# The gated unit of layer 0 in three passes of rounded and rest parts, its context loaded a batch ahead and split on GpSimd

## The chip, the core and the metric

One core of a Trainium2 chip runs the whole program. The metric is the device time of one execution in microseconds. A barrier stands between the stages of the program. TensorE (PE), VectorE (DVE), ScalarE (ACT), GpSimd (POOL) and SyncE (SP, which issues DMAs) each work through their own instructions in order and wait for one another by semaphores.

## What is computed

Two decoder layers on x of 4 batches x 512 rows x 256 features. Each layer has self-attention, a second unit over a context and a mixture of experts, each after a layer norm and added to x. In layer 0 the second unit is no attention. It is a gated unit whose three weights are all the context of the batch:

```python
def _L0_xattn_ref(x, w1, v1, w2):
    x1 = jnp.einsum('eth,efh->etf', x, w1)
    x2 = jnp.einsum('eth,efh->etf', x, v1)
    h = jax.nn.gelu(x1, approximate=True) * x2
    return jnp.einsum('etf,efh->eth', h, w2)
...
x = x + _L0_xattn_ref(_layernorm(x, axis=-1), ctx_1024, ctx_1024, ctx_1024)
```

Since w1 and v1 are the same, x1 = x2 is computed once: g = norm(x) times context transposed (512 x 256 by 256 x 512), h = gelu(g) * g, and h times context (512 x 512 by 512 x 256), for each batch.

## The kernel before

`geglu` (L805) is this unit. P is 128; a batch has NT = 4 tiles of rows, CC = 2 chunks of features and FC = 4 chunks of context rows. Features lie on partitions for the first product, context rows for the second.

One batch goes through these kinds of step, which `run` hands to each engine in the same order:

- IN: SP loads `ctxT` (the context transposed, 512 KB) and `ctxN` (the context, 512 KB) from memory, each into its only buffer. `ctxT` waits until the batch before has read it (`g_ready`), `ctxN` likewise (`y_ready`).
- LN: VectorE takes statistics and mean and variance (L978, L985). GpSimd makes the inverse deviation with two 128x4 operations (`inverse_deviation`, L968 and L970). VectorE scales the four row tiles into `xn` (L991).
- T: TensorE transposes `xn` into PSUM `t_ps` (L935), and VectorE copies that to `xnT` (L907).
- G: TensorE makes the four chunks of `g_ps` in 32-bit products (L945), two per chunk. ScalarE takes the GELU of a chunk (L921), VectorE multiplies it with g into `h` (L895).
- Y: TensorE makes the output in two halves j of two row tiles, four 32-bit products each (L956). VectorE adds a half to x (L900).

The order is LN and T of batch 0, and then for each batch b: IN(b), G(b), LN(b+1), Y(b,0), T(b+1), Y(b,1). The first three batches are a hardware loop (`batch_body`, L69), whose waits compare with values held in registers; the last follows it as straight code. So the rows of the next batch are normalised and transposed beside the output products, and everything on an engine behind a waiting instruction waits too.

The mixture of experts (`experts`, L1344) already works in three passes: each 32-bit operand is held as a rounded part (hi, type fp32r) and a rest (lo = value - hi), and hi*hi + lo*hi + hi*lo is accumulated (L1686). ScalarE rounds there (L1560) and VectorE subtracts (L1607). The tile tag `l0g` marks this unit, `l0a` the attention before it, `l0ms` and `l0m` the experts after it, and `l1a`, `l1x`, `l1m` those of layer 1.

## Time and profile before

| | us |
|---|---|
| median of 3 runs | 2181.52 |
| lowest and highest run | 2175.15, 2187.56 |
| span of the profiled execution | 2182.9 |
| of it: first attention and load of constants | 0 to 380.9 |
| of it: the gated unit, barrier to last add | 380.9 to 463.4 |
| TensorE, VectorE, ScalarE, GpSimd busy over the span | 1766.8, 1336.3, 953.7, 360.1 |

The times list holds only the three runs; the profiled execution has its span, which lies 1.4 us above their median. A busy time of an engine is a sum over stages with different limits, so the share of 81% for TensorE says little about one stage. The windows of the stage and its timeline tell which wait ends last there. A matmul's record includes the time the result takes through the array, so the distance between two starts, not the duration, is what one costs in a row of them; a 32-bit product stands in the trace as two records.

### The profile page before, as it was taken

What the parts mean: (1) busy time and instruction counts of PE and PEld (TensorE: products, weight loads), DVE (VectorE), ACT (ScalarE), POOL (GpSimd) and SP (SyncE); (2) the same over time, 40 slices, a digit from 0 to 9 for tenths busy, and PEclk for the clock granted to TensorE, in tenths of its full rate; (3) what the DMA queues carried; (4) which work ended last, traced back from release to release, by engine and by line L of the source; (5) the groups of instructions that cost most, each with busy time, mean ns of one, the idle gap of its engine ahead of it and who ended that gap; (6) DMA issues with size and microseconds to landing.
All of it is one profiled execution on the core that took longest, in us unless ns stands there. A gap on an engine that the chain in (4) does not pass through costs nothing. (4 is left out here: it accounts for less than half of the span.)

```text
span 2182.9 us, 35377 instructions
## 1 busy us (share of the span) xinstructions
PE 1766.8 (81%) x11104; PEld 1317.3 (60%) x11104; DVE 1336.3 (61%) x2397; ACT 953.7 (44%) x1769; POOL 360.1 (16%) x560
## 2 busy tenths in 40 slices
PE   4999998773979993399999958788762599999990
PEld 2566665463969993145555523333332599999990
DVE  4565663443458883577677546756874377777762
ACT  1243343111346661035455515755851366666640
POOL 4122120015000004422112022111103200000005
PEclk9799998876989996679999968988985799999995
DMA  3121110243047773212112013111104466666634
GB/s 111 35 48 42 31 45 1 58 159 104 3 131 231 231 227 96 72 40 51 31 29 58 2 51 80 46 46 39 34 1 137 142 205 208 211 210 204 206 98 120
DMA packets 193808, 211.51 MB, mean 97 GB/s; under 512 B 28723, under 2 KB 172469, under 8 KB 193717
## 3 DMA queue, kind: packets, MB, share of 16 engines
q1 hardware_dynamic: 178356, 174.71, 26.7%
q0 software_dynamic: 15360, 35.68, 6.1%
q8 instruction: 46, 0.75, 0.1%
q14 instruction: 46, 0.37, 0.1%
HBM read 143.71 MB, written 28.57 MB: 79 GB/s over the span
## 5 line engine op out<-in xcount | busy, mean ns | idle before, releaser
L1686 PE MATMUL l1m_xg_ps<-l1m_sb_xrows_hi,l1m_sb_hi 128*128 128x256 f32 x736 | 209.5, 285 | 1.4 <-DVE l1m_sb_xrows_lo L1601 1.4
L1686 PE MATMUL l1m_xg_ps<-l1m_sb_xrows_hi,l1m_sb_lo 128*128 128x256 f32 x736 | 209.2, 284 | 0.0
L1686 PE MATMUL l1m_xg_ps<-l1m_sb_xrows_lo,l1m_sb_hi 128*128 128x256 f32 x736 | 209.2, 284 | 0.0
L590 ACT ACTIVATE l1x_sb_probs<-l1x_s_ps,l1x_sb_kmax 128x512 f32<-128x512 f32 x256 | 173.6, 684 | 72.9 <-DVE l1x_sb_kmax L524 47.2
L493 DVE TENSOR_REDUCE l1a_sb_mx<-l1a_a_ps 128x1 f32<-128x512 f32 x256 | 169.2, 686 | 55.8 <-PE l1a_a_ps L666 55.1
L524 DVE TENSOR_REDUCE l1x_sb_kmax<-l1x_s_ps 128x2 f32<-128x1024 f32 x128 | 156.1, 1220 | 62.2 <-PE l1x_s_ps L693 61.8
L493 DVE TENSOR_REDUCE l0a_sb_mx<-l0a_a_ps 128x1 f32<-128x128 f32 (+3 forms) x256 | 116.4, 486 | 90.3 <-PE l0a_a_ps L669 88.3
L596 ACT ACTIVATE l1a_sb_probs<-l1a_s_ps 128x1024 f32<-128x1024 f32 x128 | 130.5, 1022 | 89.8 <-PE l1a_s_ps L693 89.3
L1686 PEld LDWEIGHTS l1m_xg_ps<-l1m_sb_xrows_hi,l1m_sb_hi 128*128 128x128 f32 x736 | 142.4, 193 | 1.8 <-DVE l1m_sb_xrows_lo L1601 1.8
L1686 PEld LDWEIGHTS l1m_xg_ps<-l1m_sb_xrows_hi,l1m_sb_lo 128*128 128x128 f32 x736 | 142.3, 193 | 0.0
L1686 PEld LDWEIGHTS l1m_xg_ps<-l1m_sb_xrows_lo,l1m_sb_hi 128*128 128x128 f32 x736 | 142.3, 193 | 0.0
L596 ACT ACTIVATE l0a_sb_probs<-l0a_s_ps 128x1024 f32<-128x1024 f32 (+3 forms) x128 | 89.6, 701 | 119.6 <-PE l0a_s_ps L696 118.9
L1607 DVE TENSOR_TENSOR l1m_sb_lo<-l1m_sb_raw,l1m_sb_hi 128x512 fp32r<-128x512 f32 x184 | 118.8, 687 | 32.5 <-ACT l1m_sb_hi L1560 30.6
L666 PE MATMUL l1a_a_ps<-l1a_sb_kst,l1a_sb_qst 96*128 96x512 f32 x256 | 130.2, 521 | 9.9 <-DVE l1a_sb_mx L493 7.3
L1560 ACT ACTIVATE l1m_sb_hi<-l1m_sb_raw 128x512 fp32r<-128x512 f32 x184 | 104.9, 620 | 16.4 <-DMA l1m_sb_raw<-in_l1m_w 15.3
L712 PE MATMUL l1x_o_ps<-l1x_sb_probs,l1x_sb_vaug 128*32 128x512 f32 x512 | 76.3, 670 | 42.8 <-DVE l1x_sb_vaug L540 42.6
L1686 PE MATMUL l1m_xy_ps<-l1m_sb_hi,l1m_sb_xh_hi 128*128 128x256 f32 x368 | 106.8, 290 | 2.8 <-issue 2.8
L1686 PE MATMUL l0m_xg_ps<-l0m_sb_xrows_hi,l0m_sb_hi 128*128 128x256 f32 x368 | 105.4, 286 | 3.1 <-DVE l0m_sb_xrows_lo L1601 3.1
L1686 PE MATMUL l0m_xg_ps<-l0m_sb_xrows_hi,l0m_sb_lo 128*128 128x256 f32 x368 | 105.1, 285 | 0.0
L1686 PE MATMUL l0m_xg_ps<-l0m_sb_xrows_lo,l0m_sb_hi 128*128 128x256 f32 x368 | 105.0, 285 | 0.0
L1686 PE MATMUL l1m_xy_ps<-l1m_sb_hi,l1m_sb_xh_lo 128*128 128x256 f32 x368 | 104.7, 285 | 0.0
L1686 PE MATMUL l1m_xy_ps<-l1m_sb_lo,l1m_sb_xh_hi 128*128 128x256 f32 x368 | 104.7, 285 | 0.0
(341 smaller groups left out, 4577.4 us busy)
## 6 DMA issues: line engine op xcount, KB each, us to landing
l1m_sb_raw<-in_l1m_w SPq DMA_DIRECT2D x184, 256.0 KB
l0m_sb_raw<-in_l0m_w SPq DMA_DIRECT2D x96, 256.0 KB
l1m_sb_raw<-in_l1m_w SPq DMA_DIRECT2D x23, 1024.0 KB
l0m_sb_raw<-in_l0m_w SPq DMA_DIRECT2D x24, 512.0 KB, 4.0
rows_dram<-const_zeros SPq DMA_DIRECT2D x1, 5888.0 KB, 22.9
l0m_sb_xrows<-rows_dram SPq DMA_DIRECT2D x23, 256.0 KB, 4.3
outs_dram<-l0m_sb_xy SPq DMA_DIRECT2D x23, 256.0 KB, 2.7
l1m_sb_xrows<-rows_dram SPq DMA_DIRECT2D x23, 256.0 KB, 3.9
```

What stands on the lines that cost most here:

```text
L493: dve.tensor_reduce(mx[:, g, qt, h:h + 1], a_ps[:, u % 2, 0:last], AX.X, ALU.max).then_inc(a_max.sem, 1)
L524: dve.tensor_reduce(kmax[:, n % 4, :], scores[buffer_of(n)][:, :, :], AX.X, ALU.max, negate=True).then_inc(kmax_done.sem, 1)
L590: ins = act.activation(probs[:, n % 8, e, :], scores[buffer_of(n)][:, e, :], ACT.Exp, bias=kmax[:, n % 4, e:e + 1], accum_out=zsum[:, n % ...
L596: act.activation(probs[:, n % 8, :, c0:T], scores[buffer_of(n)][:, :, c0:T], ACT.Exp, scale=SCALE).then_inc(exp_done.sem, 1)
L666: ins = pe.matmul(at, qst[h % 2][0:96, h // 2, qt * P:(qt + 1) * P], kst[0:96, h // 2, 0:last], start=True, stop=not causal)
L712: ins = pe.matmul(o_ps[32 * i:32 * i + 32, c0:T], vaug[:, kt, GH * g + i, :], probs[:, (8 * g + 2 * kt + i // 2) % 8, i % 2, c0:T], start= ...
L1560: ins = act.activation(two_chunks(hi, k % 2, f), two_chunks(raw13, n, f), ACT.Copy)
L1607: ins = dve.tensor_tensor(two_chunks(lo, k % 2, f), two_chunks(raw13, n, f), two_chunks(hi, k % 2, f).bitcast(F32), ALU.subtract)
L1686: ins = pe.matmul(at, s, m, start=n == 0, stop=n == len(passes) - 1)
```

## The change

In layer 0's gated unit every 32-bit product becomes three passes over fp32r parts.

- `xnT`, `h`, `ctxT` and `ctxN` each get a hi and a lo tile. ScalarE rounds (`xnT_hi` from PSUM, `h_hi` from `h`), VectorE subtracts (`xnT_lo` in place of the copy, `h_lo`).
- The context's tiles are double. Batch b + 2 is loaded after G(b) in the order, and as soon as the raw tile of batch b has been split. GpSimd splits both context tiles: cast, subtract, cast, subtract, of 128x1024 each.
- Batches 0 and 1 are split where IN stands, batch 0 ahead of LN(0) and batch 1 right behind it. Later ones are split behind the second output half, which on GpSimd is right behind the pair of LN(b+1).
- The loop over batches is gone; all four stand as straight code.
- ScalarE's table for GELU is loaded once instead of at each turn of the loop.

The diff, cut to its core:

```diff
@@ geglu: the order @@
+            step("IN", 0)
             step("LN", 0)
+            step("IN", 1)
             step("T", 0)
-            def body(b, nxt):
-                step("IN", b)
+            for b in range(B):
                 step("G", b)
-                if nxt is not None:
-                    step("LN", nxt)
+                if b + 2 < B:
+                    step("IN", b + 2)
+                if b + 1 < B:
+                    step("LN", b + 1)
                 step("Y", b, 0)
...
-            batch_body(eng, B, body)
@@ sync @@
-                wait_all(sp, (g_ready, b - 1, FC - 1))
...
+                if b >= 2:
+                    ctx_low.wait(sp, b - 2, 0)
+                sp.dma_start(ctxT[:, b % 2, :, :], w["ctxT"][b].rearrange("(c p) t -> p c t", p=P)
+                             ).then_inc(ctxT_in[b % 2], 16)
+                if b >= 2:
+                    ctx_low.wait(sp, b - 2, 1)
+                sp.dma_start(ctxN[:, b % 2, :, :], w["ctx"][b].rearrange("(c p) d -> p c d", p=P)
+                             ).then_inc(ctxN_in[b % 2], 16)
@@ gpsimd @@
+            def split(b):
+                k = b % 2
+                pool.wait_ge(ctxT_in[k], (b // 2 + 1) * 16)
+                if b >= 2:
+                    g_ready.wait(pool, b - 2, FC - 1)
+                pool.tensor_copy(ctxT_hi[:, k, :, :], ctxT[:, k, :, :]).then_inc(ctx_high.sem, 1)
+                ctx_high.wait(pool, b, 0)
+                pool.tensor_tensor(ctxT_lo[:, k, :, :], ctxT[:, k, :, :], ctxT_hi[:, k, :, :].bitcast(F32),
+                                   ALU.subtract).then_inc(ctx_low.sem, 1)
+                pool.wait_ge(ctxN_in[k], (b // 2 + 1) * 16)
+                if b >= 2:
+                    y_ready.wait(pool, b - 2, 1)
...
+            run(pool, {"LN": lambda b: inverse_deviation(pool, b, mv, rstd, const, ln_stats, ln_rstd, xn_done),
+                       "Y": lambda b, j: split(b + 2) if j == 1 and b + 2 < B else None,
+                       "IN": lambda b: split(b) if b < 2 else None})
@@ vector @@
+            def rest(b, f):
+                h_high.wait(dve, b, f)
+                dve.tensor_tensor(h_lo[:, f, :], h[:, f, :], h_hi[:, f, :].bitcast(F32), ALU.subtract
+                                  ).then_inc(h_low.sem, 1)
...
                     dve.tensor_tensor(h[:, f, :], g_ps[:, f, :], gelu[:, f, :], ALU.mult).then_inc(h_done.sem, 1)
+                    if f:
+                        rest(b, f - 1)
+                rest(b, FC - 1)
...
-                    dve.tensor_copy(xnT[:, c, :], t_ps[:, c, :]).then_inc(t_read.sem, 1)
+                    xnT_high.wait(dve, b, c)
+                    dve.tensor_tensor(xnT_lo[:, c, :], t_ps[:, c, :], xnT_hi[:, c, :].bitcast(F32), ALU.subtract
+                                      ).then_inc(t_read.sem, 1)
@@ scalar @@
+            def high(b, f):
+                h_done.wait(act, b, f)
+                y_ready.wait(act, b - 1, 1)
+                act.activation(h_hi[:, f, :], h[:, f, :], ACT.Copy).then_inc(h_high.sem, 1)
...
+                    act.activation(xnT_hi[:, c, :], t_ps[:, c, :], ACT.Copy).then_inc(xnT_high.sem, 1)
@@ tensor @@
+            def three_passes(at, chunks):
+                passes = [(s[a], m[b]) for s, m in chunks for a, b in ((0, 0), (1, 0), (0, 1))]
+                for n, (s, m) in enumerate(passes):
+                    ins = pe.matmul(at, s, m, start=n == 0, stop=n == len(passes) - 1)
+                return ins
...
-                pe.wait_ge(ctxT_in, (b + 1) * 16)
+                ctx_low.wait(pe, b, 0)
...
-                    pe.wait_ge(ctxN_in, (b + 1) * 16)
-                    h_done.wait(pe, b, FC - 1)
+                    ctx_low.wait(pe, b, 1)
+                    h_low.wait(pe, b, FC - 1)
```

GpSimd at the start of the unit, before: the pair of batch 0, then the loop (L72 and L57 are the loop's and the waits' own instructions) with the pair of the next batch.

```order
L880 UNCONDITIONAL_BRANCH
L968 TENSOR_TENSOR l0g_sb_rstd<-l0g_sb_mv,const_eps 128x4
L970 TENSOR_TENSOR l0g_sb_rstd<-l0g_sb_rstd,const_minus_half 128x4
L72 UNCONDITIONAL_BRANCH
L72 ISA
L57 ISA
L968 TENSOR_TENSOR l0g_sb_rstd<-l0g_sb_mv,const_eps 128x4
L57 ISA
L970 TENSOR_TENSOR l0g_sb_rstd<-l0g_sb_rstd,const_minus_half 128x4
```

The same place of the changed kernel: the splits of batches 0 and 1, and the pairs of batches 0 and 1.

```order
L903 CAST l0g_sb_ctxT_hi<-l0g_sb_ctxT 128x1024
L905 TENSOR_TENSOR l0g_sb_ctxT_lo<-l0g_sb_ctxT,l0g_sb_ctxT_hi 128x1024
L910 CAST l0g_sb_ctxN_hi<-l0g_sb_ctxN 128x1024
L912 TENSOR_TENSOR l0g_sb_ctxN_lo<-l0g_sb_ctxN,l0g_sb_ctxN_hi 128x1024
L1035 TENSOR_TENSOR l0g_sb_rstd<-l0g_sb_mv,const_eps 128x4
L1037 TENSOR_TENSOR l0g_sb_rstd<-l0g_sb_rstd,const_minus_half 128x4
L903 CAST l0g_sb_ctxT_hi<-l0g_sb_ctxT 128x1024
L905 TENSOR_TENSOR l0g_sb_ctxT_lo<-l0g_sb_ctxT,l0g_sb_ctxT_hi 128x1024
L910 CAST l0g_sb_ctxN_hi<-l0g_sb_ctxN 128x1024
L912 TENSOR_TENSOR l0g_sb_ctxN_lo<-l0g_sb_ctxN,l0g_sb_ctxN_hi 128x1024
L1035 TENSOR_TENSOR l0g_sb_rstd<-l0g_sb_mv,const_eps 128x4
L1037 TENSOR_TENSOR l0g_sb_rstd<-l0g_sb_rstd,const_minus_half 128x4
```

Four operations of 128x1024 have come ahead of the first pair, and four between it and the second.

VectorE through G and LN, before, in the last (straight) batch and the add behind it: four multiplies in a row, and nothing after them but the adds. In the loop the same four stand ahead of the statistics of the next batch.

```order
L72 REGISTER_ALU
L72 COMPARE_AND_BRANCH
L895 TENSOR_TENSOR l0g_sb_h<-l0g_g_ps,l0g_sb_gelu 128x512 x4
L900 TENSOR_TENSOR x_sb<-l0g_y_ps,x_sb 128x512 x2
L808 UNCONDITIONAL_BRANCH
```

Changed, G(0) and LN(1) on VectorE:

```order
L935 TENSOR_TENSOR l0g_sb_h<-l0g_g_ps,l0g_sb_gelu 128x512 x2
L926 TENSOR_TENSOR l0g_sb_h_lo<-l0g_sb_h,l0g_sb_h_hi 128x512
L935 TENSOR_TENSOR l0g_sb_h<-l0g_g_ps,l0g_sb_gelu 128x512
L926 TENSOR_TENSOR l0g_sb_h_lo<-l0g_sb_h,l0g_sb_h_hi 128x512
L935 TENSOR_TENSOR l0g_sb_h<-l0g_g_ps,l0g_sb_gelu 128x512
L926 TENSOR_TENSOR l0g_sb_h_lo<-l0g_sb_h,l0g_sb_h_hi 128x512 x2
L1045 BN_STATS l0g_sb_stats<-x_sb 128x6 x4
L1050 MEMSET l0g_sb_nothing 128x1
L1052 BN_AGGR l0g_sb_mv<-l0g_sb_stats 128x2 x4
L1058 TENSOR_SCALAR l0g_sb_xn<-x_sb,l0g_sb_mv,l0g_sb_rstd 128x256 x4
```

Each chunk's subtraction stands behind the next chunk's multiply, and the last two stand ahead of the statistics and scalings of the next batch. On TensorE the unit had 64 products and transposes as code (8 transposes, a loop body of 32, 24 after it) and has 320 now (4 times 8 + 24 + 48).

## Rows read from the trace of the kernel before

**Rows 1.** Windows of the unit: busy us (x instructions) by engine, PEclk, DMA share, GB/s

```profile
387.10:395.90 8.80, 7.91 (x15) 4.09 (x16) 1.43 (x3) 1.88 (x2) 0.00 (x0) 0.50 0.00 1
395.90:463.60 67.70, 56.69 (x210) 36.88 (x208) 29.34 (x69) 11.31 (x17) 3.62 (x6) 1.00 0.17 47
```

**Rows 2.** Chain that ended last, in order of time: start, us, what

```profile
1812.95 8.64 PE l1m_xg_ps L1686 x72
```

**Rows 3.** Timeline of turn 1: start, us, engine, line, operation, count, [idle before <-releaser]

```profile
411.19 7.03 PE L945 MATMUL l0g_g_ps<-l0g_sb_xnT,l0g_sb_ctxT 128*128 128x512 f32 x16
418.33 0.60 ACT L921 ACTIVATE l0g_sb_gelu<-l0g_g_ps 128x512 f32<-128x512 f32 x1 [1.12 <-PE l0g_g_ps L945]
419.57 1.39 DVE L978 BATCH_NORM_STATS2 l0g_sb_stats<-x_sb 128x6 f32 x4
419.79 3.72 PE L956 MATMUL l0g_y_ps<-l0g_sb_ctxN,l0g_sb_h 128*128 128x256 f32 x16 [1.57 <-DVE l0g_sb_h L895]
424.72 1.09 PE L935 MATMUL l0g_t_ps<-const_ident,l0g_sb_xn 128*128 128x128 f32 x8 [1.22 <-DVE l0g_sb_xn L991]
429.10 7.03 PE L945 MATMUL l0g_g_ps<-l0g_sb_xnT,l0g_sb_ctxT 128*128 128x512 f32 x16
```

**Rows 4.** Timeline, start and end of the unit

```profile
382.35 0.43 SPq L873 DMA_DIRECT2D l0g_sb_ctxT<-in_ctxT  x1
384.28 0.20 POOL L968 TENSOR_TENSOR l0g_sb_rstd<-l0g_sb_mv,const_eps 128x4 f32<-128x4 f32 x1 [70.68 <-DVE l0g_sb_mv L985]
384.56 1.03 POOL L970 TENSOR_TENSOR l0g_sb_rstd<-l0g_sb_rstd,const_minus_half 128x4 f32<-128x4 f32 x1
385.69 1.38 DVE L991 TENSOR_SCALAR l0g_sb_xn<-x_sb,l0g_sb_mv,l0g_sb_rstd 128x256 f32<-128x256 f32 x4 [1.49 <-issue]
389.96 10.10 PE L945 MATMUL l0g_g_ps<-l0g_sb_xnT,l0g_sb_ctxT 128*128 128x512 f32 x16 [0.86 <-DVE l0g_sb_xnT L907]
401.63 3.72 PE L956 MATMUL l0g_y_ps<-l0g_sb_ctxN,l0g_sb_h 128*128 128x256 f32 x16 [1.57 <-DVE l0g_sb_h L895]
455.50 7.14 PE L956 MATMUL l0g_y_ps<-l0g_sb_ctxN,l0g_sb_h 128*128 128x256 f32 x32 [1.46 <-issue]
462.69 0.69 DVE L900 TENSOR_TENSOR x_sb<-l0g_y_ps,x_sb 128x512 f32<-128x512 f32 x1 [2.76 <-PE l0g_y_ps L956]
```

**Rows 5.** Groups by line (count, busy, mean ns, idle), then one DMA issue group (us to landing)

```profile
L1560 ACT ACTIVATE l1m_sb_hi<-l1m_sb_raw 128x512 fp32r<-128x512 f32 x184 | 104.9, 620 | 16.4 <-DMA l1m_sb_raw<-in_l1m_w 15.3
L413 POOL TENSOR_TENSOR l1a_sb_vaug<-l1a_sb_v,l1a_sb_bv 128x256 f32<-128x256 f32 x16 | 11.8, 740 | 3.9 <-PE l1a_o_ps L712 2.7 <-issue 1.0
L387 POOL MEMSET l1a_sb_vaug<- 128x2048 f32 x1 | 1.8, 1837 | 0.1
...
l0g_sb_ctxT<-in_ctxT SPq DMA_DIRECT2D x4, 512.0 KB, 3.6
```

**Rows 6.** Timeline, GpSimd and VectorE, start of the first layer and at 1120 us

```profile
12.85 3.50 POOL L383 MEMSET l0a_sb_qst<- 128x4096 f32 x1
12.98 9.32 DVE L450 TENSOR_SCALAR l0a_sb_xn<-x_sb,l0a_sb_mv,l0a_sb_rstd 128x256 f32<-128x256 f32 x4 [1.51 <-issue]
...
1119.96 1.46 POOL L413 TENSOR_TENSOR l1a_sb_vaug<-l1a_sb_v,l1a_sb_bv 128x256 f32<-128x256 f32 x2
1119.74 1.84 DVE L450 TENSOR_SCALAR l1a_sb_xn<-x_sb,l1a_sb_mv,l1a_sb_rstd 128x256 f32 x2
```

**Rows 7.** Timeline of TensorE: longest and shortest of the five gaps

```profile
1395.31 1.23 PE L712 MATMUL l1x_o_ps<-l1x_sb_probs,l1x_sb_vaug 128*32 128x512 f32 x8 [3.22 <-DVE l1x_sb_vaug L540]
...
2122.99 0.44 PE L1686 MATMUL l1m_xy_ps<-l1m_sb_hi,l1m_sb_xh_hi 128*128 128x256 f32 x1 [2.85 <-issue]
```

**Rows 8.** Windows behind those two gaps

```profile
1395.80:1402.40 6.60, 6.50 (x29) 2.80 (x21) 4.69 (x9) 5.53 (x16) 2.53 (x5) 0.52 0.26 65
2123.20:2126.40 3.20, 3.20 (x16) 3.20 (x16) 0.00 (x0) 0.00 (x0) 0.00 (x0) 0.50 0.00 0
```

**Rows 9.** Waits of TensorE: line, cause, us in total, times, longest

```profile
PE l0ms_xg_ps L1686 <- issue: 19.7, 16, 2.4
```

More of the change, by code:

```diff
@@ L822, in geglu @@
         xn = sb("xn", [P, NT, D])
-        xnT = sb("xnT", [P, CC, T])
-        ctxT = sb("ctxT", [P, CC, T])
-        ctxN = sb("ctxN", [P, FC, D])
+        xnT_hi, xnT_lo = (sb(n, [P, CC, T], F32R) for n in ("xnT_hi", "xnT_lo"))
+        ctxT = sb("ctxT", [P, 2, CC, T])
+        ctxN = sb("ctxN", [P, 2, FC, D])
+        ctxT_hi, ctxT_lo = (sb(n, [P, 2, CC, T], F32R) for n in ("ctxT_hi", "ctxT_lo"))
+        ctxN_hi, ctxN_lo = (sb(n, [P, 2, FC, D], F32R) for n in ("ctxN_hi", "ctxN_lo"))
         gelu = sb("gelu", [P, FC, T])
         h = sb("h", [P, FC, T])
+        h_hi, h_lo = (sb(n, [P, FC, T], F32R) for n in ("h_hi", "h_lo"))
         nothing = sb("nothing", [P, 1])
@@ L832, in geglu @@
         y_ps = ps("y_ps", [P, 2, 2, D])
-        ctxT_in = ctx.enter_context(nc.semaphore(f"{tag}_ctxT_in"))
-        ctxN_in = ctx.enter_context(nc.semaphore(f"{tag}_ctxN_in"))
+        ctxT_in = [ctx.enter_context(nc.semaphore(f"{tag}_ctxT_in{k}")) for k in range(2)]
+        ctxN_in = [ctx.enter_context(nc.semaphore(f"{tag}_ctxN_in{k}")) for k in range(2)]
         ln_stats = steps("ln_stats", 2 * NT)
@@ L921, in gate, with transposed @@
                     act.activation(gelu[:, f, :], g_ps[:, f, :], ACT.Gelu_apprx_tanh).then_inc(g_gelu.sem, 1)
-            run(act, {"G": gate})
+                    if f:
+                        high(b, f - 1)
+                high(b, FC - 1)
+            def transposed(b):
+                for c in range(CC):
+                    t_ready.wait(act, b, c)
+                    g_ready.wait(act, b - 1, FC - 1)
+                    t_read.wait(act, b - 1, c)
+                    act.activation(xnT_hi[:, c, :], t_ps[:, c, :], ACT.Copy).then_inc(xnT_high.sem, 1)
+            run(act, {"G": gate, "T": transposed})
         @block.tensor
@@ L943, in hidden @@
                     h_done.wait(pe, b - 1, f)
[L944 to L947 removed]
+                    cols = slice(f * P, (f + 1) * P)
+                    three_passes(g_ps[:, f, :], [((ctxT_hi[:, b % 2, c, cols], ctxT_lo[:, b % 2, c, cols]),
+                                                  (xnT_hi[:, c, :], xnT_lo[:, c, :])) for c in range(CC)]
+                                 ).then_inc(g_ready.sem, 1)
             def output(b, j):
                 if j == 0:
[L951 to L952 removed]
+                    ctx_low.wait(pe, b, 1)
+                    h_low.wait(pe, b, FC - 1)
                 x_added.wait(pe, b - 1, j)
                 for t in range(2):
[L955 to L957 removed]
+                    rows = slice((2 * j + t) * P, (2 * j + t + 1) * P)
+                    ins = three_passes(y_ps[:, j, t, :], [((h_hi[:, f, rows], h_lo[:, f, rows]),
+                                                           (ctxN_hi[:, b % 2, f, :], ctxN_lo[:, b % 2, f, :]))
+                                                          for f in range(FC)])
                 ins.then_inc(y_ready.sem, 1)
```

37 lines of the change are left out of this document (17 added, 20 removed).

## The prediction

> **What bounds the kernel now.** The kernel is a chain of stages with a barrier between them, so a microsecond won or lost inside one stage shows in full at the end unless a later wait takes it up. I first read the windows of the gated unit [rows 1], then a whole turn of its loop in the timeline [rows 3], then its start and end [rows 4]. The unit fills 380.9 to 463.4 us, 82.5 of 2182.9 us. From 395.9 us on TensorE's clock is 1.00, the 2.4 GHz level; before that it is 0.50. One turn runs from 411.19 to 429.10 us, 17.91 us, and TensorE sets most of it. The hidden products take 7.03 us. Then it waits 1.57 us for the last GELU and product, and starts the first half of the output products at 419.79. It next waits 1.22 us for the normalised rows of the next batch (transposes at 424.72), and does the second output half [rows 3]. GpSimd has little to do here: two tiny operations per batch, the second 1.03 us long, yet every batch's transposes wait behind them [rows 4].
>
> **The products.** A 32-bit hidden product appears as two records, 16 for a batch in 7.03 us. In three passes it is 24 of 512 columns. In the experts, which already work in three passes, a 256-column pass costs 8.64/72 = 0.120 us [rows 2]. One of 512 columns costs twice that at most, 0.24, and half a 32-bit record of the same width, 7.03/16/2 = 0.22, is the nearest row below [rows 3]. I take 0.22: 24 x 0.22 = 5.3 us; with 0.24 it would be 5.8, and the gate chain below ends no later than 0.2 us after. The output is 48 passes of 256 columns, 5.76 us, where 32 records took 7.14 [rows 4]. Alone that would save 1.7 + 1.4 us a batch, 12 us in all. What follows takes it back.
>
> **Gate chain.** Before, the last product of a group is followed by one GELU (0.60) and one multiply (0.69). Now a rounding copy on ScalarE (0.62) and a subtraction on VectorE (0.69) follow [rows 3, 5], and each engine does two operations per chunk. VectorE's pace is then 2 x 0.69 = 1.38 us plus hops, about 1.42, against TensorE's 1.32. Stepping through the four chunks from the start of G, with the result read 0.28 us after the last pass: results at 1.6, 2.9, 4.3, 5.6; last multiply ends 7.2, last rounding 7.8, last rest 8.6. Output begins at 8.7 us. Before it was 419.79 - 411.19 = 8.60 [rows 3]. So the quicker hidden products buy nothing (+0.1), and TensorE now stands idle about 3.2 us there instead of 1.57. The saved output half before the transposes buys nothing either: they wait for normalised rows, which follow the gate chain. Only the half after them shortens: 429.10 - 424.72 = 4.39 becomes 0.93 + 2.88 = 3.81, a gain of 0.6 a turn.
>
> **The split stands ahead of the first normalisation.** In GpSimd's order four 128x1024 operations now precede the 1/deviation of batch 0. The nearest rows are its 128x256 add, 740 ns, and its 128x2048 memset, 1837 ns [rows 5]. The 128x4 add takes 0.20 us (0.28 from 384.28 to 384.56), so the add grows by (0.74 - 0.20)/252 = 2.15 ns per element and a subtraction of 1024 is 2.45 us. A cast has one input: at the memset's 0.9 ns it is 0.95 us, at the adding rate 2.45. I take 1.3, nearer the memset. The context is issued at 382.35 and lands 3.6 to 3.9 us later, 386.2 [rows 4, 5]. Then 2 x (1.3 + 2.45) + gaps 0.3 + the pair 1.3 ends at 395.3, against 385.59 before: **+9.7 us**. Bounds: 0.95 and 2.2 give +8.5; all four at 3.0 give +14.2.
>
> By the Trainium skill (GPSIMD Engine Reference, section Elementwise — side-by-side cycle accounting) a two-input operation on 2048 elements takes 4497 ns there, which as an estimate is 2.25 us for 1024. With it the sum below would be 1.2 us lower. No run so far shows a 1024-element operation.
>
> **GpSimd holds VectorE.** At the first layer's start, four VectorE scalings of 128x256 take 9.32 us, though one takes 0.35 to 0.41 alone. Beside them GpSimd runs memsets one after another, the first of 3.50 us and a later one of 1.84 [rows 4 to 6]. At 1119.74 two scalings take 1.84 us beside two GpSimd adds [rows 6]. This is the same operation as `xn`, from the same kind of operands. In the new order a split stands right behind the pair of batch 0, 1 and 2, and its inputs are there by then, so it starts with the scalings. Batch 0 meets all four operations (7.5 us + 0.4 instead of 1.38): **+6.5**. Batches 1 and 2 meet cast and subtraction of ctxT; the ctxN half waits for output that itself waits for these rows: 3.75 + 0.1 + two free scalings 0.7 + the tail 0.35 = 4.9 instead of 1.38, **+3.5** each. Batch 3 meets none. The bound below is 0 if VectorE always gets in first; above, with 3.0 us operations, +11 and +5.9.
>
> **Clock.** In stretches at 1.00, idle gaps of TensorE of 1.6 us did not lower it. The five gaps from 2.85 to 3.22 us all did: two of them with the clock behind are shown [rows 7, 8]. It stays at 0.50, the 1.2 GHz level, for over 3 us after work resumes at 2122.99 and for some 7 at 1395.31 [rows 7, 8]. The new 3.2 us gap and, in turns 0 and 1, some 4 us before the transposes are such gaps. A fall in the first output half is covered by the wait for the rows. A fall at the transposes or in the last output is not: 4 us at half speed do 2 us of work, **+2.0**, three times.
>
> **Sum, against the profile's own time.** To the first output: +9.7 + 6.5, one more hop through ScalarE between transposes and products +0.6, and the first hidden products, partly at the low clock both times, with their chain 10.95 instead of 401.63 - 389.96 = 11.67 [rows 4], -0.7: **+16.1**. Turns 0 and 1: 3.5 + 2.0 - 0.6 + 0.1 = 5.0 each, **+10.0**. Turn 2: -0.6 + 0.1 = **-0.5**. End: 463.38 - 455.50 = 7.88 becomes 5.76 + 0.36 + 0.69 + 2.0 = 8.8, **+0.9**. Total +26.5 us. The three dropped table loads (1.28 us) lay behind running products in the loop and cost or give nothing; the first one stays. The earlier context loads are hidden both times after batch 0. The span of 2182.9 stands 1.4 above the median of the runs, so the sum gives 2181.5 + 26.5 = **2208 us**.
>
> **Rivals.**
> *A dear cast* (0.13). If casts and subtractions take 3.0 us each, the bounds above add 4.5 + 4.5 + 2 x 2.4 = 14: 2222 us. For it: a rounding copy may be software work per element; against it: the memset's rate.
> *No holding* (0.10). If only memsets and adds into that buffer hold VectorE, or it always gets in first, 6.5 + 7.0 and the two clock falls at the transposes go, 17.5 less: 2190.5 us. Against it stands the 1.84 us beside adds [rows 6].
> *Not slower, by a stall that moves* (0.10). In the next stage TensorE waits 19.7 us in 16 gaps for nothing the profile shows, between 525 and 550 us, while GpSimd scatters rows [rows 9]. The unit's straight code grows from 64 to 320 TensorE products and transposes, which shifts all code behind it. If the stall depends on where the code lies, it can go: with the clock's part of it 22 us, 2208 - 22 = 2186. It decides from the point where less than 12 us of the terms above remain or more than 15 of the stall goes. Against it: it begins and ends with the scatter, which moves along unchanged. It could also grow, by up to the scatter's remaining 20 us.
> The Trainium skill (Runtime: NRT & Kernel Launch, section Instruction fetch mechanics) says that instructions are refilled in blocks of 256, so a shift of the code moves the block ends; it also advises unrolling over loops. No row shows a wait at the end of the present loop, so by the trace the unrolling gives nothing here.
>
> **Numbers.** The forecast has 0.60 with 2200 to 2216 as its own range, the rivals 0.13, 0.10 and 0.10; 0.07 is left for gains I can't name, such as a gate chain that hides better. Leaving out what lies beyond them on both sides, the range is 2190 to 2222. A measurement of this kernel can tell some 0.5% (11 us) from no change: slower needs over 2192.4. Slower by more: 0.60 + 0.13 and 0.02 of the others, 0.75. Within: *no holding* and most of the moved stall, 0.20. Faster by more: 0.05, if the stall goes and nothing holds VectorE.
>
> **What would show it.** The first pair of 128x4 operations of the unit should end near 395 us after the four splits; `l0g_sb_xn` should have a median near 0.4 us but a maximum of several us, for batches 0 to 2 alone; TensorE's gap before the first output product should be 3.0 to 3.3 us, with the clock at 0.50 behind it; the unit should last about 109 us. The forecast falls if the cast takes under 1 us and the scalings keep 0.41 us, or if the waits between 525 and 550 us change.

## The result and the profile after

| | before | after |
|---|---|---|
| median, us (10 runs each, timed in turn) | 2186.69 | 2200.04 |
| lowest and highest, us | 2175.15, 2192.97 | 2196.68, 2206.14 |
| span of the profiled execution, us | 2182.9 | 2197.8 |
| the unit, us | 83.2 | 102.4 |

The changed kernel is slower: ratio 1.0076, 95% interval 1.0056 to 1.0095, which is 12 to 21 us. Over ten runs the kernel before has a median 5.2 us above that of the three runs that the forecast started from, so the medians differ by 13.4 us. "The unit" is measured here and below from the start of the last addition of the attention before it (L516 on VectorE) to the end of the unit's own last addition. It grew by 19.2 us where the forecast had 26.5. All splits, holds and clock falls that the prediction named are there, most of them smaller.

The start, from the timeline of the changed kernel (start, us, engine, line, operation, count, idle before and its releaser). It answers [rows 4]:

```profile
387.19 1.04 POOL L903 CAST l0g_sb_ctxT_hi<-l0g_sb_ctxT 128x1024 fp32r<-128x1024 f32 x1 [69.35 <-DMA l0g_sb_ctxT<-in_ctxT]
388.30 2.34 POOL L905 TENSOR_TENSOR l0g_sb_ctxT_lo<-l0g_sb_ctxT,l0g_sb_ctxT_hi 128x1024 fp32r<-128x1024 f32 x1
...
394.28 1.03 POOL L1037 TENSOR_TENSOR l0g_sb_rstd<-l0g_sb_rstd,const_minus_half 128x4 f32<-128x4 f32 x1
395.28 1.03 POOL L903 CAST l0g_sb_ctxT_hi<-l0g_sb_ctxT 128x1024 fp32r<-128x1024 f32 x1
395.40 6.94 DVE L1058 TENSOR_SCALAR l0g_sb_xn<-x_sb,l0g_sb_mv,l0g_sb_rstd 128x256 f32<-128x256 f32 x4 [9.74 <-issue]
...
402.39 1.97 PE L994 MATMUL l0g_t_ps<-const_ident,l0g_sb_xn 128*128 128x128 f32 x8 [20.87 <-DVE l0g_sb_xn L1058]
```

The split starts when the context lands, four operations pass, and the pair of 128x4 operations ends at 395.31. The next split starts at once, beside the four scalings, which take 6.94 us instead of 1.38. TensorE sits idle for 20.87 us.

A turn is the time from one batch's first output product to the next's. The first line below is of the kernel before, where the scalings of the next batch take 1.38 us and start 3.64 us behind their statistics (419.57 in [rows 3]); the others are the same part of turn 0 in the changed kernel:

```profile
423.21 1.38 DVE L991 TENSOR_SCALAR l0g_sb_xn<-x_sb,l0g_sb_mv,l0g_sb_rstd 128x256 f32 x4 [1.51 <-POOL l0g_sb_rstd L970]
...
416.75 0.36 PE L1002 MATMUL l0g_y_ps<-l0g_sb_ctxN_hi,l0g_sb_h_hi 128*128 128x256 f32 x1 [2.85 <-issue]
419.71 1.03 POOL L903 CAST l0g_sb_ctxT_hi<-l0g_sb_ctxT 128x1024 fp32r<-128x1024 f32 x1
419.85 4.12 DVE L1058 TENSOR_SCALAR l0g_sb_xn<-x_sb,l0g_sb_mv,l0g_sb_rstd 128x256 f32<-128x256 f32 x4 [1.47 <-issue]
420.82 2.34 POOL L905 TENSOR_TENSOR l0g_sb_ctxT_lo<-l0g_sb_ctxT,l0g_sb_ctxT_hi 128x1024 fp32r<-128x1024 f32 x1
424.02 1.55 PE L994 MATMUL l0g_t_ps<-const_ident,l0g_sb_xn 128*128 128x128 f32 x8 [2.67 <-DVE l0g_sb_xn L1058]
```

Two gaps stand here, 2.85 us ahead of the output and 2.67 ahead of the transposes; batch 1 has the same again (2.85, 2.66 and scalings of 4.12 us), batches 2 and 3 only the gap ahead of the output. Windows behind them (columns as in [rows 1]) show the clock; those of before are 1.00 in the same two places:

```profile
417.80:421.30 3.50, 3.50 (x18) 3.35 (x16) 1.99 (x8) 0.00 (x0) 2.68 (x4) 0.53 0.01 2
424.50:427.70 3.20, 3.20 (x17) 3.20 (x16) 1.45 (x3) 1.19 (x2) 0.00 (x0) 0.50 0.00 0
```

TensorE's issue waits in the experts stage, which answer [rows 9], hardly changed:

```profile
PE l0ms_xg_ps L1753 <- issue: 18.5, 14, 3.2
```

### The profile page after: what moved, and what is told of

It is laid out like the page before. It is cut to its first block and busy times, and to the rows that moved or that the text cites. A ratio compares the mean times of both kernels' runs of the same rounds, so it can differ in the third digit from the quotient of the medians.

```text
span 2197.8 us, 35505 instructions
## 1 busy us (share of the span) xinstructions
PE 1759.5 (80%) x11200; PEld 1327.4 (60%) x11200; DVE 1356.9 (62%) x2413; ACT 964.0 (44%) x1791; POOL 387.9 (18%) x576
## 5 line engine op out<-in xcount | busy, mean ns | idle before, releaser
L712 PE MATMUL l1x_o_ps<-l1x_sb_probs,l1x_sb_vaug 128*32 128x512 f32 x512 | 75.3, 662 | 42.1 <-DVE l1x_sb_vaug L540 41.8
```

Of the source, the lines that this page charges most:

```text
L712: ins = pe.matmul(o_ps[32 * i:32 * i + 32, c0:T], vaug[:, kt, GH * g + i, :], probs[:, (8 * g + 2 * kt + i // 2) % 8, i % 2, c0:T], start= ...
```

## Experiments

Theory: the loss is (a) the split ahead of the first pair, (b) GpSimd's large operations holding VectorE's scalings, (c) the clock behind the gaps; the saved products buy little because the gate chain sets the output's start. The rivals: no holding, a gap that has nothing to do with the split, a stall elsewhere that moves. Each experiment starts from the changed kernel unless it says otherwise. e1 to e4 ran on one chip (before 2184.67 us), e5 to e7 on a second (2152.75), e8, e6 again, e9 and e10 on a third (2178.65), e11 on a fourth (2183.47).

### e1: the first pair ahead of the split

```diff
-            step("IN", 0)
             step("LN", 0)
+            step("IN", 0)
             step("IN", 1)
```

> The changed kernel with one swap in the common order: LN(0) stands ahead of IN(0), so GpSimd makes the 1/deviation of batch 0 before it splits any context. Theory 1 (the split ahead of the pair and its holding of VectorE cost the start 13.8 us): the pair no longer waits for the context, which lands about 4.3 us after the last add of the attention plus 1.3; the first cast starts with the second scaling, so the four scalings still take about 5 us (one of them free), and the products of batch 0 start some 10 us earlier than in the changed kernel: the unit takes 91 to 92 us instead of 101.7, the turns stay at 21.1, 21.0 and 16.8 us. Rival (the start is late because the products must wait for the split context in any order): the products of batch 0 start no more than 2 us earlier and the unit keeps over 99 us.

Unit 92.4 us, 10.0 less. The first hidden product came 10.3 us earlier.

```profile
383.52 1.03 POOL L1037 TENSOR_TENSOR l0g_sb_rstd<-l0g_sb_rstd,const_minus_half 128x4 f32<-128x4 f32 x1
384.65 4.92 DVE L1058 TENSOR_SCALAR l0g_sb_xn<-x_sb,l0g_sb_mv,l0g_sb_rstd 128x256 f32<-128x256 f32 x4 [1.48 <-issue]
384.79 1.16 POOL L903 CAST l0g_sb_ctxT_hi<-l0g_sb_ctxT 128x1024 fp32r<-128x1024 f32 x1 [0.24 <-DMA l0g_sb_ctxT<-in_ctxT]
```

The pair ends 8.3 us earlier, measured from the start of the unit. The other 2.0 us come from a shorter hold (4.92 us for 6.94), because the first scaling starts ahead of the first cast and is free. So the place of the split costs 8.3 us, and the scalings are held as soon as a split stands beside them. The whole time was 2201.15 in one run, no lower than that of the changed kernel: layer 1's two attention stages took 733.9 us in that execution and 720.3 in the changed kernel's. The experiments are therefore read from the unit first; e9 and e10 are about this.

### e2: a split waits for the scalings

```diff
                 k = b % 2
+                if b:
+                    xn_done.wait(pool, b - 1, NT - 1)
                 pool.wait_ge(ctxT_in[k], (b // 2 + 1) * 16)
```

> The changed kernel, but GpSimd starts the split of batch 1, 2 and 3 only when VectorE has finished scaling the rows of the batch before (a wait on xn_done added, the order kept). Theory 1 (GpSimd's operations hold VectorE's scalings, and the late rows then let the clock fall): the four scalings take 1.4 us for every batch, 5.6 us less at the start and 2.7 less in turns 0 and 1; the gap before the transposes goes below 2 us, the clock stays up there, and turns 0 and 1 come down from 21.1 to about 16.8 us. The unit takes 87 to 88 us instead of 101.7. Rival (the scalings are slow for another reason, such as the context's DMAs writing into SBUF beside them): they keep 6.9 and 4.1 us and the unit keeps over 99 us.

Unit 87.9 us, whole time 2191.65. Scalings of this kernel (min/median/max, ns):

```profile
L1060 DVE TENSOR_SCALAR l0g_sb_xn<-x_sb,l0g_sb_mv,l0g_sb_rstd x16: 403/407/412, 393.0 to 446.1; 128x256 f32<-128x256 f32 x16
```

No scaling is longer than 0.412 us; in the changed kernel the longest of the 16 took 2.507. Turns 0 and 1 fell from 21.1 to 16.8 us, which turn 2 had before. So the hold is real, and with it the gap before the transposes and its clock fall are gone: 14.5 us of the unit for one wait, 5.6 of them at the start and 8.5 in the two turns. *No holding* falls.

### e3: both edits

e1's order, and no split beside scalings, not even the first:

```diff
                 k = b % 2
+                xn_done.wait(pool, max(b - 1, 0), NT - 1)
                 pool.wait_ge(ctxT_in[k], (b // 2 + 1) * 16)
```

> Both edits of the two runs beside it: the pair of batch 0 ahead of every split, and every split, that of batch 0 too, waits for the scalings of the batch before it in the order. Theory 1: products of batch 0 start within 1.5 us of where they start in the kernel before, three turns of about 16.8 us, and an end with one fall of the clock: a unit of 79 to 80 us against 82.5 before and 101.7 in the changed kernel. The time is 2 to 4 us under the kernel before, 0.999, hardly to be told from it, and about 20 under the changed kernel. Rival (the three passes cost by themselves, by twice the work on ScalarE and VectorE): the unit stays over 86 us.

2180.01 us over 12 runs, ratio 0.9975 to before, interval 0.9953 to 0.9998. Unit 81.5 us: 20.9 less than the changed kernel, 1.7 less than before in its first profile but only 0.2 less than in its second (81.7, e10), so the unit alone doesn't tell the two apart. I had expected 79 to 80. The first output came 12.28 us after the first hidden product, where the changed kernel has 10.93. This is where the subtractions of the rests (`h_lo`) of the first batch stand:

```profile
397.35 2.67 POOL L913 TENSOR_TENSOR l0g_sb_ctxN_lo<-l0g_sb_ctxN,l0g_sb_ctxN_hi 128x1024 fp32r<-128x1024 f32 x1
398.43 2.74 DVE L927 TENSOR_TENSOR l0g_sb_h_lo<-l0g_sb_h,l0g_sb_h_hi 128x512 fp32r<-128x512 f32 x2
```

Two `h_lo` take 2.74 us instead of 1.47, beside a split; e8 and e11 take this up.

### e4: the gaps filled with products nobody reads

```diff
+            def fill(at, n):
+                for _ in range(n):
+                    pe.matmul(at, xnT_hi[:, 0, 0:P], xnT_hi[:, 0, 0:D], start=True, stop=True)
...
                 if j == 0:
                     ctx_low.wait(pe, b, 1)
+                    x_added.wait(pe, b - 1, 0)
+                    fill(y_ps[:, 0, 0, :], 23)
...
+                if b:
+                    t_read.wait(pe, b - 1, CC - 1)
+                    fill(t_ps[:, 0, 0:D], 28 if b < 3 else 14)
                 xn_done.wait(pe, b, NT - 1)
```

> The changed kernel with products nobody reads put into TensorE's two gaps: 23 passes of 256 columns between the hidden products and the first output half (into y_ps, which the output then overwrites), and 28 or 14 before the transposes (into t_ps). They are as long as the gaps, so nothing waits for them that did not wait before. Theory 1 (gaps of 2.85 us let the clock fall, and its fall costs some 1.5 us at the transposes of batches 1 and 2 and 1.5 to 2 in the last output): the granted clock stays 1.00 from about 411 us to the end of the unit, the first output half takes 2.9 us instead of 4.6, transposes to next products take 3.8 instead of 5.2 us in turns 0 and 1, the end 6.9 instead of 8.2, and the unit takes 96 to 98 us instead of 101.7. Rival (the clock falls for some other reason, or its fall is hidden everywhere): the clock still falls, or the unit keeps 101 us or more.

Unit 97.9 us, 4.4 less. The clock stayed at the 2.4 GHz level:

```profile
417.00:430.00 13.00, 12.12 (x81) 10.96 (x80) 8.68 (x13) 4.75 (x9) 5.28 (x3) 1.00 0.01 1
430.00:446.00 16.00, 15.07 (x113) 14.18 (x112) 10.90 (x21) 2.60 (x5) 7.11 (x6) 1.00 0.00 1
```

From the end of a turn's scalings to its first hidden product it is now 3.9 us, against 5.4 in the changed kernel. One fall is worth 1.5 us, three times, where the prediction took 2.0.

### e7: one pass instead of three

The rest passes are left out; all roundings, splits and subtractions stay.

```diff
-                passes = [(s[a], m[b]) for s, m in chunks for a, b in ((0, 0), (1, 0), (0, 1))]
+                passes = [(s[a], m[b]) for s, m in chunks for a, b in ((0, 0),)]
```

> The changed kernel in which TensorE makes only the first of the three passes (rounded by rounded) of the unit's hidden and output products and leaves the two with the rests out; every split, rounding and subtraction on the other engines stays. TensorE's products in the unit fall to a third. Theory 1 and 2 (the engines around TensorE set the turn: gate chain, then normalised rows): hidden products to first output shrink only from 8.6 to about 7.3 us (four multiplies and four rests of 1.38 us each pair, behind a first GELU 0.8 us after the start), turns 0 and 1 lose about 1.3 us there and 1.9 behind the transposes, more if less work means less time at the low clock; unit 89 to 94 us instead of 101.7. Rival (TensorE's passes set the turn): a turn falls by more than half of the 7 us taken away, unit under 87 us.

Unit 88.0 us, slightly below the 89 that I had as the lower end. TensorE's gaps take up most of what the products give back:

```profile
430.11 2.05 PE L1002 MATMUL l0g_y_ps<-l0g_sb_ctxN_hi,l0g_sb_h_hi 128*128 128x256 f32 x8 [4.86 <-issue]
437.36 1.97 PE L994 MATMUL l0g_t_ps<-const_ident,l0g_sb_xn 128*128 128x128 f32 x8 [5.21 <-DVE l0g_sb_xn L1058]
```

The gaps grow from 2.85 to 4.86 and from 2.67 to 5.21, and turns 0 and 1 lose only 2.7 us each. Two thirds of TensorE's product work is worth 14 of 102 us, half of it (7.4) between first hidden product and first output and in the last output. In the turns the stage is set by the chain through VectorE and GpSimd.

### e6: the kernel before, normalised two batches ahead

If the turn is set by the chain G, gate, statistics, pair, scalings, transposes, the cure doesn't need three passes. The kernel before, as straight code, in another order:

```diff
             step("T", 0)
+            step("LN", 1)
-            def body(b, nxt):
+            for b in range(B):
                 step("IN", b)
                 step("G", b)
-                if nxt is not None:
-                    step("LN", nxt)
+                if b + 1 < B:
+                    step("T", b + 1)
+                if b + 2 < B:
+                    step("LN", b + 2)
                 step("Y", b, 0)
-                if nxt is not None:
-                    step("T", nxt)
                 step("Y", b, 1)
-            batch_body(eng, B, body)
```

> The kernel before, in 32-bit products, in the same new order and as straight code: LN two batches ahead, T(b+1) right behind G(b), single context buffers. Theory 2: the gate chain is 8.6 us here too, then two output halves of 3.5 us: turns of 15.6 to 16 us, unless the context's DMA of the next batch is late. Its buffer for the hidden products is free from the end of G(b) on, so it is not. The unit takes 75 to 77 us, 6 us under the kernel before (0.997), and 2 to 4 us more than the three-pass kernel in this order: that difference is all the three passes are worth. Rival (the new order gains nothing without the early context and the split): turns stay at 17.5 us or more.

2142.59 us, ratio to before 0.9957, interval 0.9929 to 0.9986. Unit 75.6 us, turns 15.47 where the kernel before has 17.8 to 18.2.

```profile
415.31 1.04 PE L935 MATMUL l0g_t_ps<-const_ident,l0g_sb_xn 128*128 128x128 f32 x8
...
416.93 7.14 PE L956 MATMUL l0g_y_ps<-l0g_sb_ctxN,l0g_sb_h 128*128 128x256 f32 x32 [0.59 <-issue]
...
423.91 7.03 PE L945 MATMUL l0g_g_ps<-l0g_sb_xnT,l0g_sb_ctxT 128*128 128x512 f32 x16
```

The transposes fill the gap while the gate chain ends, and the output runs in one piece. The edit changes two things at once, the order and the loop, and no run has the straight code in the old order. What the traces show of the loop is small: 0.4 us a turn between statistics and scalings (3.64 us in the loop, 3.27 here). The expectation that three passes in this order would be 2 to 4 us faster still is answered by e5 and e8, and it did not come true. Repeated on the third chip:

> The kernel before with 32-bit products, unrolled, normalised two batches ahead, the same code as in the experiment with the norm ahead in the kernel before. It is timed beside the three-pass kernel in the same order. If three passes gain nothing over 32-bit products once the order is the same, the two differ by less than 3 us (unit 75.6 here). If the pass count matters in this stage, the three-pass kernel is 5 us or more ahead. Against the kernel before: 7 to 10 us less, as measured on the other chip.

2173.45 us, ratio 0.9976 (0.9959 to 0.9994), unit 75.4: 5.2 us less than before, not 7 to 10. The three-pass kernel timed beside it (e8) is 5.7 us slower, so neither of the two cases came true. Three passes cost something in e8, and e11 shows most of what.

### e5: the same order with three passes

e3 in e6's order, with both output halves in one go:

```diff
             step("IN", 1)
             step("T", 0)
+            step("LN", 1)
...
-                xn_done.wait(pool, max(b - 1, 0), NT - 1)
+                xn_done.wait(pool, b if b >= 2 else 0, NT - 1)
```

> On top of the version with both edits (pair first, splits wait for the scalings), the order is changed: LN runs two batches ahead, and T(b+1) comes right behind G(b) on every engine, so TensorE transposes the next batch in the gap of the gate chain and then makes both output halves in one go. Theory 2 (a turn is the gate chain of 8.6 us, then whatever TensorE does until it can start the next hidden products; three passes gain only what stands behind that chain): a turn is 8.6 + 5.8 = 14.4 to 15 us instead of 17.9 before, the unit about 72 to 74 us against 82.5, the time 8 to 11 us under the kernel before (0.995 to 0.996). Rival (the two operations per chunk on ScalarE and VectorE make the engines that copy and subtract the bound, or the splits of GpSimd collide with scalings or rests in the new order): turns of 16.5 us or more and no more than 4 us under the kernel before.

A miss: 2151.0 us, ratio 1.000 (0.9974 to 1.0025), and the unit 84.4 us. Turns 0 and 1 were 16.6 us from output to output and turn 2 14.3, and the first output came 18.2 us behind the first hidden product. In turns 0 and 1 the rival came true as well: one `h_lo` in each, of 1.51 and 1.77 us, stood beside a split.

```profile
399.71 1.01 POOL L1039 TENSOR_TENSOR l0g_sb_rstd<-l0g_sb_rstd,const_minus_half 128x4 f32<-128x4 f32 x1
400.81 1.38 DVE L1060 TENSOR_SCALAR l0g_sb_xn<-x_sb,l0g_sb_mv,l0g_sb_rstd 128x256 f32<-128x256 f32 x4 [10.04 <-issue]
402.11 1.28 DVE L937 TENSOR_TENSOR l0g_sb_h<-l0g_g_ps,l0g_sb_gelu 128x512 f32<-128x512 f32 x2
```

The statistics of batch 1 were ready at 390.8, but its pair stands behind both splits on GpSimd. VectorE waited 10.04 us for it, and the gate products of batch 0 stood behind it in VectorE's queue: the fault of the change once more, one batch later.

### e8: the pair of batch 1 between the two splits

From e5:

```diff
             step("LN", 0)
             step("IN", 0)
-            step("IN", 1)
             step("T", 0)
             step("LN", 1)
+            step("IN", 1)
```

Every split now waits for the scalings of its own batch.

> All of the computation is done, as in the three-pass kernel with the norm two batches ahead; only the order on GpSimd differs: the pair of batch 1 now stands between the split of batch 0 and the split of batch 1, and each split waits for the scalings of its own batch. Theory: the first turn of the norm-ahead kernel was long (25.8 us against 16.3 and 15.1 of the others) because the 1/deviation of batch 1 stood behind eight large GpSimd operations, its scalings came 16.5 us after those of batch 0, and VectorE, in order, held the gate products of batch 0 behind them. Then here the scalings of batch 1 should start 9 to 10 us after those of batch 0 (four large operations, 7.0 us, and the pair), the first turn should fall from 25.8 to 17 to 19 us, turns 1 and 2 should stay at 15 to 16.5, and the unit, from the start of the last addition before it, should last 75 to 78 us instead of 84.4. Rival: the three-pass gate chain itself is what makes the first turn long, because the clock is at 0.50 in the first hidden products; then the first turn stays above 23 us and the unit above 82. Whole time against the kernel before by the first: 6 to 9 us less.

Mostly a miss. The scalings of batch 1 started 9.7 us after those of batch 0, as expected, but the first turn (here from hidden product to hidden product, as in the expectation) fell only from 25.8 to 22.6 us. The unit took 83.9 us, and the whole 2179.18 (ratio 1.0004, 0.9987 to 1.0021). The rival, a clock at 0.50 in the first products, explains it no better: those of before and of e6 are at that level too. GpSimd and VectorE in the first gate chain:

```profile
397.92 2.37 POOL L907 TENSOR_TENSOR l0g_sb_ctxT_lo<-l0g_sb_ctxT,l0g_sb_ctxT_hi 128x1024 fp32r<-128x1024 f32 x1
398.04 2.81 DVE L928 TENSOR_TENSOR l0g_sb_h_lo<-l0g_sb_h,l0g_sb_h_hi 128x512 fp32r<-128x512 f32 x1
400.24 1.50 POOL L912 CAST l0g_sb_ctxN_hi<-l0g_sb_ctxN 128x1024 fp32r<-128x1024 f32 x1
400.77 0.68 DVE L937 TENSOR_TENSOR l0g_sb_h<-l0g_g_ps,l0g_sb_gelu 128x512 f32<-128x512 f32 x1
401.82 2.67 POOL L914 TENSOR_TENSOR l0g_sb_ctxN_lo<-l0g_sb_ctxN,l0g_sb_ctxN_hi 128x1024 fp32r<-128x1024 f32 x1
402.81 2.83 DVE L928 TENSOR_TENSOR l0g_sb_h_lo<-l0g_sb_h,l0g_sb_h_hi 128x512 fp32r<-128x512 f32 x2
```

One `h_lo` takes 2.81 us instead of 0.68 and ends at 400.85, its own 0.6 us after GpSimd's subtraction. The multiply at 400.77, which reads PSUM, keeps 0.68 beside a cast. GpSimd pays too: the cast took 1.50 instead of 1.04. The Trainium skill (SBUF — State Buffer, section Who interferes with whom) says that VectorE and GpSimd share one pair of SBUF ports, that a VectorE instruction with two SBUF inputs contends for it with a GpSimd instruction that reads SBUF, that `tensor_scalar` can too, and that whoever comes second "fully blocks" until the other is done. The rows agree on who is held: `h_lo` (two SBUF inputs) and the scalings are, the multiply (one input in PSUM) is not, nor are the statistics (one input), which take 1.40 us at 416.56 in the changed kernel with GpSimd idle and 1.40 at 390.36 here with it busy. Whether a held scaling is blocked from its first element they don't show: it ends 0.15 us behind GpSimd's operation, where a free one takes 0.40.

### e11: splits wait for the rests too

From e8:

```diff
                 xn_done.wait(pool, b, NT - 1)
+                if b:
+                    h_low.wait(pool, b - 1, FC - 1)
                 pool.wait_ge(ctxT_in[k], (b // 2 + 1) * 16)
```

> All of the computation is done. Against the three-pass kernel whose pair of batch 1 stands between the splits, one wait is added: from batch 1 on a split on GpSimd starts only when VectorE has made the last h_lo of the batch before. In that kernel the h_lo subtractions, whose operands all lie in SBUF, took up to 2.81 us instead of 0.68 while GpSimd was splitting, and the multiplies, which read PSUM, kept 0.69. Theory: GpSimd's large operations hold those of VectorE's operations that work from SBUF alone, and this is what ate the gain. Then every h_lo should take 0.68 to 0.70 us here, the first output product should come 11.4 to 11.9 us after the first hidden product instead of 15.1, turn 0 (from first output product to first output product) 15.3 to 16 us instead of 16.6, and the unit 77 to 80 us instead of 83.9. Rival: the long h_lo was VectorE waiting for the rounding on ScalarE, shown as duration; then h_lo stays up to 2.8 us and the unit stays above 82.5. What may go the other way: the pair of batch 3 now stands behind a later split, and its scalings may delay the additions; I expect no more than 1 us from it.

2173.08 us, ratio to before 0.9956, interval 0.9929 to 0.9984. The unit took 75.3 us, 8.6 less than e8, and the first output came 11.4 us after the first hidden product. All rests of this kernel:

```profile
L930 DVE TENSOR_TENSOR l0g_sb_h_lo<-l0g_sb_h,l0g_sb_h_hi x16: 677/682/693, 399.2 to 449.1; 128x512 fp32r<-128x512 f32 x16
```

So the hold made the `h_lo` long, and the rival falls. Of the 8.6 us, 3.7 lie between first hidden product and first output and 0.8 in turns 0 and 1. The other 4.1 are two places where e8's clock was at 0.50 and e11's was not: the output of batch 2 (1.5) and that of batch 3 (2.7). That this, too, follows from the hold is not shown. It is also why the unit came out below the expected 77 to 80. Windows of e11 behind the gaps ahead of its four outputs (columns as in [rows 1]):

```profile
402.90:406.00 3.10, 2.80 (x15) 2.83 (x16) 3.06 (x12) 0.45 (x1) 2.69 (x2) 0.65 0.02 5
419.00:422.00 3.00, 2.62 (x18) 2.65 (x19) 2.96 (x11) 0.53 (x2) 2.52 (x2) 0.81 0.02 5
435.00:438.00 3.00, 2.44 (x20) 2.47 (x21) 1.66 (x3) 0.71 (x2) 2.34 (x2) 1.00 0.00 0
449.00:457.00 8.00, 5.99 (x48) 5.81 (x48) 2.07 (x3) 0.04 (x1) 0.00 (x0) 1.00 0.01 2
```

Turns 0 and 1 took 16.2 us each, a little over the 15.3 to 16 expected. The pair of the batch after next stands behind a split, and VectorE waits 5.50 us for it:

```profile
411.53 1.38 DVE L1062 TENSOR_SCALAR l0g_sb_xn<-x_sb,l0g_sb_mv,l0g_sb_rstd 128x256 f32<-128x256 f32 x4 [5.50 <-issue]
```

That wait costs 0.4 us a turn, from hidden product to output 8.86 us instead of 8.48. Turn 2, without it and with the clock at 1.00 in its output, took 14.3. This is the best three-pass kernel here and beats both kernels of the case; the 32-bit one of e6 does the same (0.9957 and 0.9976, unit 75.6 and 75.4) with less code and one tile for each context where this one has six.

### e9 and e10: the two kernels once more

> The changed kernel unaltered, profiled once more. The unit should last 102.4 us again, to 0.3. Theory: layer 1's two attention stages vary by several us between executions of one kernel. Then their sum, 720.3 us in the first profile of this kernel and between 713 and 734 in those of the others, should differ from 720.3 by more than 2 us here. Rival: their length belongs to the kernel, where its code lies; then it is 720.3 to 0.5.

> The kernel before unaltered, profiled once more on the same chip as the others of this group. Unit 83.2 us again, to 0.3. The sum of layer 1's attention stages was 726.3 us in its first profile; by the theory that it varies between executions it differs by more than 2 us, by the rival that it belongs to the code it is 726.3 to 0.5. The issue waits of TensorE in the experts after the unit were 19.7 us in 16 gaps on the first chip; if they belong to the chip and not to the code, this profile and that of the changed kernel here have them both or lack them both.

The changed kernel's unit was 102.5 us again (2202.85 in one run), that of before 81.7, 1.5 less than in its first profile. That is a miss: the first output came 10.1 us after the first hidden product, not 11.7, since the clock was at 1.00 from 2.9 us behind that product on and not from 6.0. The two attention stages of layer 1, first transposes to those of the experts, together took 726.3 and 729.6 us before, 720.3 and 725.4 after. So their length varies by 3 to 5 us between executions of one kernel. It accounts for the span: +19.2 in the unit, +1.4 ahead of it and -6.0 in these two stages are +14.6 of the +14.9 us. Two things stay open. Both pairs of profiles have the stages shorter in the changed kernel, by 6.0 and 4.2 us, and e1's 733.9 us, which hide its gain, lie 8 to 14 us above the two of the changed kernel. Whether that is the execution or the place of the code, no run here tells.

The issue waits of [rows 9] were 20.6 us for before and 13.7 for after here, and lay between 12.6 (e11) and 21.3 (e4) in all profiles on the first, third and fourth chip. On the second chip e5, e6 and e7 had none at all, and the stage from its first products to those of the next took 85 to 86 us instead of 113 to 116. Three different codes lack the waits on that chip, and e6's own code has them on the third (18.3 us). So they go with the chip or where the program lies on it, and not with the unit's edit; which of the two, no run here tells.

## Why the prediction was right, and where its terms were off

| step, us against before | forecast | measured |
|---|---|---|
| split ahead of the first pair | +9.7 | +8.35 |
| scalings of batch 0 held | +6.5 | +5.55 |
| hop through ScalarE | +0.6 | +0.6 |
| first hidden products and gate chain | -0.7 | -0.74 |
| turns 0 and 1, each | +5.0 | +2.9, +3.1 |
| turn 2 | -0.5 | -1.0 |
| end | +0.9 | +0.35 |
| the unit | +26.5 | +19.2 |

**Direction and mechanisms held.** The kernel is slower by what the prediction named, in the places it named. e1 shows the split ahead of the pair (8.3 of its 10.3 us), e2 the hold with the gap behind it (14.5), e4 the clock (4.4), e7 that TensorE's work is not the bound in the turns. The time, 2200.04, lies 8 us under the forecast and at the lower edge of its own range, 2200 to 2216.

**The total was nearer than the sum.** The forecast put 26.5 us on a base of 2181.5, the median of three runs. On the ten-run median of 2186.69 the same sum would have said 2213, 13 us too high. The measured change is 13.4 us by the medians and 16.6 by the ratio. So part of the small distance is luck in the base. The opening premise, that a microsecond won or lost in the unit shows in full at the end, failed in part too: the unit grew by 19.2 us (20.8 in e9 and e10), the whole by less. What is missing lies in layer 1's attention stages, and why is open, as said above.

**The split** was mis-sized by 1.35. The cast took 1.04 us, not 1.3, and the subtraction 2.34, not 2.45 (my own rate of 2.15 ns gives 2.39 for 1024 elements; 2.45 was a slip); the memset's rate of 0.9 ns per element was the right neighbour for a cast. *A dear cast* falls. The Trainium skill's figure (GPSIMD Engine Reference, section Elementwise — side-by-side cycle accounting) gave an estimate of 2.25 for the subtraction: nearer than my 2.45, 4% short of the measured one.

**The hold** was mis-sized by 0.8 to 1.0 us each time: 6.94 us instead of 7.9 for batch 0, 4.12 instead of 4.9 for the others. Much of that is the same two durations: with 1.04 and 2.34 my own sum gives 7.2 and 4.5. The rest, 0.2 to 0.4 us, is the tail that I added. The single scalings of batch 0 took 1.06, 2.49, 1.12 and 2.50 us beside operations of 1.03, 2.34, 1.10 and 2.34: each held scaling ends 0.15 us behind the one GpSimd operation beside it, and no further scaling follows the last one. In batch 1 two are held (1.04, 2.51) and two are free (0.40 each).

**The turns** carry most of the rest, 4.0 of 7.3. By parts of turn 1: from output to transposes +2.3 instead of +3.5 (0.8 for the shorter hold, and 0.4 because the straight code takes 3.27 us from the start of the statistics to the scalings, where the loop took 3.64; I had said that the unrolling gives nothing); from transposes to hidden products +0.9 instead of +1.4 (the clock fall costs 1.5, as e4 shows, not 2.0); from these to the output -0.1 instead of +0.1 (the chain took 8.47 us, and the gap 2.85 where I had 3.0 to 3.3). That gap is as short as the shortest of [rows 7], and the clock fell behind it in all four batches.

**The first gate chain** agrees by chance: -0.74 against the first profile of the kernel before, but +0.66 between e10 and e9, where the clock of before rose sooner.

**The end** was +0.35: the last half ran at the low level for less of its length than I took.

**The stall that moves** didn't: 18.5 us in 14 waits after, 19.7 in 16 before, and the stage took 114.2 us in both (113.3 and 115.2 in e9 and e10). The Trainium skill says (Runtime: NRT & Kernel Launch, section Instruction fetch mechanics) that instructions are refilled in blocks of 256; no cost of a shift of the block ends is visible here, though the code behind the unit lies elsewhere.

**The signs.** The first pair ended at 395.31, as said. The median of `xn` was 0.73 us and not near 0.4, since 8 of the 16 scalings were held, as my own working counts them. The gap was 2.85 us for 3.0 to 3.3, the unit 102.4 us for 109. Of the three table loads two went, not three.

**The rule on the clock was wrong as it stood.** I had said that gaps of 1.6 us don't lower it. The trace of the kernel before has two gaps of 1.68 us of TensorE, ending at 1411.86 and 1498.25, each in a stretch at 1.00. Behind the first the clock stayed at 1.00, behind the second it was at 0.50:

```profile
1411.90:1415.00 3.10, 3.10 (x14) 1.17 (x14) 1.12 (x2) 0.26 (x1) 0.00 (x0) 1.00 0.23 53
1498.60:1501.80 3.20, 3.20 (x5) 1.15 (x4) 0.00 (x0) 0.00 (x0) 0.00 (x0) 0.50 0.22 52
```

The forecast was not hurt by it, because all four gaps of 2.85 us were followed by a fall; e11 has one that was not.

**What it missed.** That a hold is a matter of operands. I had it as a thing of the scalings, and so neither e3's nor e8's expectation counted `h_lo`. In the changed kernel it cost nothing, since no split ran beside a gate chain (all 16 took 0.68 to 0.69 us), and the forecast was safe by that accident.

## What to carry over

Before work is moved to GpSimd, list for each large operation there what runs on VectorE beside it, and what stands behind it in GpSimd's own queue: a tiny operation that others wait for goes ahead of it, and the VectorE operations that were held here (subtractions with both inputs in SBUF, scalings from SBUF to SBUF) don't go beside it. One wait that keeps the two engines apart can be worth more (14.5 us here) than the products that the move was to save. And where a stage is a chain, try the order first: with the norm two batches ahead, 32-bit products take 75 us, and three passes take the same 75 only once no split stands beside a held operation.

## What the runs showed of the hardware beyond that

- GpSimd takes 1.04 us for a cast of 128x1024 to fp32r and 2.34 for a subtraction with two inputs, and both grow when an `h_lo` of VectorE has started first (1.50 and 2.67, e8).
- The length of a single gap does not tell whether the clock falls. In the changed kernel it fell within about 1 us of work resuming behind all four gaps of 2.85 us. In e11 it was at 0.65 and 0.81 in the windows behind gaps of 2.33 and 2.36 us and at 1.00 behind those of 2.37 and 2.85. In e5 it was at 0.50 behind one of 2.48 us and at 1.00 behind one of 2.74. What else decides is open. Dummy products in the gaps kept it at 1.00 (e4).
- The kernel before took 2152.75 us on one chip and 2178.65 to 2186.69 on the others. For e6's code, which was profiled on the fast chip and on a slower one, 29 us of the difference lie in the experts stage with its issue waits (86.0 against 114.6 us), absent on the faster chip.
